# A fused attention and expert kernel, closed by a block without GpSimd's drain

## The chip, the cores and the metric

The kernel runs on one core of a Trainium2 chip. Times are device microseconds (us) of one execution. Three runs of the kernel before took 154.77, 157.05 and 154.83 us, median 154.83 us. A further execution was taken with the hardware profiler.

## What is computed

Tokens x (64 sequences of 64 tokens, 128 wide, f32) go through one gated cross-attention step and one gated mixture-of-experts step:

```python
x = x + tanh(g_xattn[0]) * xattn(layernorm(x), ctx, ctx, Wq, bq, Wk, bk, Wv, bv)
x = x + tanh(g_ffn[0]) * ffn(layernorm(x), Wr, br, W1, W2)
# ffn, for each token h: route = sigmoid(h @ Wr + br); e = argmax(route)
#                        out = max(route) * (gelu(h @ W1[e]) @ W2[e])
```

There are 8 experts with W1 of 128 x 512 and W2 of 512 x 128, and each token goes to one of them.

## The kernel before, in words

The program is written engine by engine, with explicit semaphores, inside one block (`block = stack.enter_context(nc.Block())`). Within the block each of the five engines has its own instruction list: SyncE (SP) issues loads, ScalarE (ACT) and VectorE (DVE) do activations, copies and normalisation, TensorE (PE) does the matmuls, and GpSimd (POOL) does small vector operations and all the indirect DMAs. The 4096 tokens are 32 tiles of 128 rows, in 8 groups of 4.

In the first part each group is normalised, attends, and is routed; GpSimd then writes each of its 4 tiles into a DRAM buffer `scratch`, sorted by expert, with an indirect DMA (`scatter_rows`, line 408, 32 of them). In the second part 39 expert tiles are loaded back from `scratch` by SP, pass through two matmul layers, and GpSimd writes each finished tile to its rows of the output with an indirect DMA (`scatter_tile`, line 433, 39 of them; each adds 16 to the semaphore `tok_out`). Between two of these indirect DMAs GpSimd executes `pause()`, a memset of an unused tile (line 427). Nothing follows the last `scatter_tile` in GpSimd's list.

The last instruction in SP's list is a wait for all 39 output DMAs:

```python
            sp.wait_ge(tok_out, 16 * FFN_TILES)
```

Behind the lists the block closes. In the kernel before, each engine there branches to a common end, executes a DRAIN, and passes a barrier of all engines made of semaphore events. The profile puts these instructions down to line 74, the `with ExitStack() as stack:` that closes the block. A similar barrier stands at the program's start (line 1276). No computation comes behind the block.

Of the kernel before, what the change touches and what calls it, by code (L numbers as in the profile page):

```python
# [31 lines left out]
def attention_moe(nc, x, ctx_in, g_xattn, g_ffn, Wq, bq, Wk, bk, Wv, bv, Wr, br, W1, W2, out):  # L32
# [41 lines left out]
    with ExitStack() as stack:  # L74
# [206 lines left out]
        def lead(j):  # L281
            return 3 if j < 7 else 2

        block = stack.enter_context(nc.Block())

        @block.sync
        def _(sp):
# [999 lines left out]
```

## Time and profile before

| | |
|---|---|
| median of 3 runs | 154.83 us |
| lowest and highest run | 154.77 and 157.05 us |
| the profiled execution's own time | 155.01 us |
| its span, first to last instruction | 153.1 us |
| time of that execution outside its span | 1.91 us |
| mean granted TensorE clock | 0.975 |

The profile is one execution. Busy times count the work of an engine's datapath; an instruction that only the engine's sequencer executes (branch, semaphore event, DRAIN) is not counted as busy, and is listed with a q behind the engine's name (POOLq, SPq, PEldq). Where one line is queried, each row gives the shortest, median and longest duration of an instruction in ns and the start of the first and the last in us from the start of the span. A row of the chain of waits gives start, duration and instruction.

### The profile page before, as it was taken

To read this page: it belongs to the slowest core of one execution; us is meant where nothing else is said; L and a number is where in the kernel's file an instruction comes from. 1 tells how busy PE (TensorE), PEld (TensorE's weight loads), DVE (VectorE), ACT (ScalarE), POOL (GpSimd) and SP (SyncE) were. 2 spreads that over 40 slices of the span, in tenths; PEclk is the share of its full clock that TensorE was granted. 3 is DMA by queue.
4 is the path that set the end of the run, shared out by engine and by line. 5 is a ranking of instruction groups with operands and counts; after the bars stand their busy time and mean duration, and the time that the engine had idled before them with its cause. 6 is when DMAs were issued, how large, how long until landed. Compare 5 with 4: busy or idle time off the path is not lost.

```text
span 153.1 us, 4237 instructions
## 1 busy us (share of the span) xinstructions
PE 128.3 (84%) x1225; PEld 114.4 (75%) x1225; DVE 96.4 (63%) x542; ACT 77.7 (51%) x174; POOL 126.0 (82%) x209
## 2 busy tenths in 40 slices
PE   5999989998987958697599999999999999996000
PEld 5877856875774938697589998999999999995000
DVE  0699999879999997897198454454554454542000
ACT  0657397668658472628225555456546555431000
POOL 6539996898987988798989989989899898998930
PEclk9999999999999999999999999999999999999955
DMA  4999999631111241411243144544110101111000
GB/s 111 251 279 275 333 330 295 188 103 42 35 35 40 61 101 39 107 35 57 72 106 94 35 125 124 122 125 111 51 39 22 50 17 55 35 36 35 0 0 0
DMA packets 20080, 15.20 MB, mean 99 GB/s; under 512 B 6606, under 2 KB 16978, under 8 KB 20058
## 3 DMA queue, kind: packets, MB, share of 16 engines
q1 hardware_dynamic: 17328, 10.59, 26.5%
q0 software_dynamic: 2272, 4.27, 8.3%
q8 instruction: 11, 0.18, 0.5%
q10 hardware_dynamic: 458, 0.08, 0.3%
q14 instruction: 11, 0.09, 0.2%
HBM read 10.12 MB, written 5.26 MB: 100 GB/s over the span
## 4 chain that ended last, share of the span: by engine, by line
PE 43%; POOL 36%; issue 6%; DVE 5%; DMA 3%; ACT 1%; SPq 1%; POOLq 0%; DVEq 0%
PE banks_o L1172 20%; POOL scratch L408 15%; PE banks_v L1163 9%; POOL unused L427 6%; POOL rows L404 5%; PE bank_q L1163 5%; PE bank_p L1163 4%; POOL xn L369 3%; POOL out_dram L433 3%; POOL mv L362 3%; PE bank_x L1155 3%; PE bank_s L1039 2%; DMA scratch<-rows,row_at 1%; DMA tok<-scratch 1%; DVE stats L587 1%
## 5 line engine op out<-in xcount | busy, mean ns | idle before, releaser
L1172 PE MATMUL banks_o<-w_sb,hT 128*128 x312 | 41.8, 277 | 0.7 <-issue 0.5
L1172 PEld LDWEIGHTS banks_o<-w_sb,hT 128*128 128x128 f32 x312 | 37.9, 192 | 1.7 <-issue 1.6
L408 POOL DMA_INDIRECT scratch<-rows,row_at x32 | 31.8, 994 | 5.7 <-issue 5.0
L905 DVE SCALAR_TENSOR_TENSOR tok<-banks_o,tok 128x128 f32<-128x128 f32 x39 | 13.6, 348 | 29.6 <-PE banks_o L1172 29.2
L427 POOL MEMSET unused<- 128x400 f32 x64 | 29.4, 459 | 0.1
L480 ACT COPY w_now<-w_sb 128x512 f32 x39 | 23.7, 612 | 4.6 <-issue 4.6
L433 POOL DMA_INDIRECT out_dram<-tok,token_at x22 | 21.6, 982 | 3.7 <-issue 3.2
L1163 PE MATMUL banks_v<-toknT,w_now 128*128 128x128 f32 x160 | 21.1, 275 | 0.0
L894 DVE TENSOR_SCALAR tokn<-tok 128x128 f32<-128x128 f32 x39 | 18.4, 472 | 2.9 <-DMA tok<-scratch 2.9
L1163 PEld LDWEIGHTS banks_v<-toknT,w_now 128*128 128x128 f32 x160 | 19.4, 192 | 0.0
L433 POOL DMA_INDIRECT out_dram<-tok x17 | 16.7, 982 | 2.9 <-issue 2.4
L537 ACT ACTIVATE hT<-banks_v 128x512 f32<-128x512 f32 x20 | 12.0, 598 | 13.8 <-PE banks_v L1163 13.8
L1155 PE MATMUL bank_x<-ident,tokn 128*128 128x128 f32 x39 | 11.0, 283 | 4.9 <-DVE tokn L894 3.9
L901 DVE COPY toknT<-bank_x 128x128 f32<-128x128 f32 x39 | 11.2, 286 | 1.3 <-PE bank_x L1155 1.3
L362 POOL TENSOR_TENSOR mv<-mv,minus_half 128x4 f32<-128x4 f32 x8 | 8.2, 1020 | 4.6 <-DVE mv L595 4.6
L677 DVE SCALAR_TENSOR_TENSOR rows<-banks_o,inv_sum,x_all 128x136 f32<-128x136 f32 x32 | 10.9, 352 | 0.0
L404 POOL TENSOR_TENSOR rows<-rows,minus_half 128x4 f32<-128x4 f32 x8 | 8.3, 1040 | 2.9 <-DVE rows L742 2.7
L1163 PE MATMUL bank_q<-toknT,w_now 128*128 128x128 f32 x80 | 10.6, 276 | 0.0
L524 ACT ACTIVATE probs<-bank_s,minus_max 128x64 f32<-128x64 f32 x32 | 7.4, 315 | 5.9 <-DVE minus_max L641 5.9
L537 ACT ACTIVATE hT<-bank_q 128x512 f32<-128x512 f32 x10 | 5.9, 593 | 8.4 <-PE bank_q L1163 8.4
L1155 PEld LDWEIGHTS bank_x<-ident,tokn 128*128 128x128 f32 x39 | 5.6, 142 | 6.1 <-DVE tokn L894 6.0
L1163 PEld LDWEIGHTS bank_q<-toknT,w_now 128*128 128x128 f32 x80 | 9.7, 192 | 0.0
(162 smaller groups left out, 252.9 us busy)
## 6 DMA issues: line engine op xcount, KB each, us to landing
tok<-scratch SPq DMA_DIRECT2D x39, 66.0 KB, 2.1
x_all<-in_x_dram SPq DMA_DIRECT2D x8, 256.0 KB, 4.5
w_sb<-in_L_ffn_W_dram SPq DMA_DIRECT2D x1, 2048.0 KB
ctx<-in_ctx_dram SPq DMA_DIRECT2D x8, 128.0 KB, 4.5
scratch<-pad_rows SPq DMA_DIRECT2D x1, 528.0 KB, 19.5
scratch<-rows,row_at POOLq DMA_INDIRECT x32, 2.4
out_dram<-tok,token_at POOLq DMA_INDIRECT x22
out_dram<-tok POOLq DMA_INDIRECT x17
```

What stands on the lines that cost most here:

```text
L362: nc.gpsimd.tensor_tensor(rstd, var, minus_half[:].unsqueeze(2), ALU.pow).then_inc(rstd1_ready, 1)
L404: nc.gpsimd.tensor_tensor(column(g, RSTD), column(g, RSTD), minus_half[:].unsqueeze(2), ALU.pow).then_inc(rstd2_ready, 1)
L408: nc.gpsimd.indirect_dma_start(out=scratch, out_offset=bass.IndirectOffsetOnAxis(ap=row_at[:, g * GT + t:g * GT + t + 1], axis=0), in_=row ...
L427: nc.gpsimd.memset(unused[:], 0.0).then_inc(paused, 1)
L433: nc.gpsimd.indirect_dma_start(out=out_tok, out_offset=bass.IndirectOffsetOnAxis(ap=at, axis=0), in_=tok[j][:, 0:D], in_offset=None, bound ...
L480: nc.scalar.copy(w1_now[j % DEEP][:], w1_sb[:, bass.ds(w_at[j], F)]).then_inc(w1_copied, 1)
L537: nc.scalar.activation(hT[j % DEEP][:], h_ps[j % DEEP], ACT.Gelu).then_inc(gelu_done, 1)
L894: nc.vector.tensor_scalar(tokn[j % 2][:], tok[j][:, 0:D], tok[j][:, MEAN:RSTD], tok[j][:, RSTD:SCALE], ALU.subtract, ALU.mult).then_inc(to ...
L905: nc.vector.scalar_tensor_tensor(out=tok[j][:, 0:D], in0=y_ps[j % 2], scalar=tok[j][:, SCALE:TOKEN], in1=tok[j][:, 0:D], op0=ALU.mult, op1 ...
L1155: nc.tensor.transpose(tT_ps, tokn[j % 2][:], ident[:]).then_inc(toknT_done, 1)
L1163: last = nc.tensor.matmul(h_ps[j % DEEP][:, c * P:(c + 1) * P], w1_now[j % DEEP][:, c * P:(c + 1) * P], toknT[j % DEEP][:], start=True, st ...
L1172: last = nc.tensor.matmul(y_ps[j % 2], hT[j % DEEP][:, c * P:(c + 1) * P], w2_sb[:, bass.ds(w_at[j] + c * D, D)], start=(c == 0), stop=(c ...
```

## The change

The block is built with an option that leaves out GpSimd's DRAIN at its end. The other four engines still drain, and the engines still meet in a barrier of semaphore events. The lists of instructions inside the block stay as they are.

```diff
-        block = stack.enter_context(nc.Block())
+        block = stack.enter_context(nc.Block(no_gpsimd_drain=True))
```

## Rows read from the trace of the kernel before

**Rows 1.** The page: its head, and each engine's busy time, share and instructions.
```profile
span 153.1 us, 4237 instructions
...
PE 128.3 (84%) x1225; PEld 114.4 (75%) x1225; DVE 96.4 (63%) x542; ACT 77.7 (51%) x174; POOL 126.0 (82%) x209
```

**Rows 2.** Busy time of each engine in three stretches at the end.
```profile
core 0: us, PE busy (x) PEld busy (x) DVE busy (x) ACT busy (x) POOL busy (x), PEclk, DMA share, GB/s
136.00:139.20 3.20, 3.20 (x30) 3.14 (x29) 0.55 (x5) 1.19 (x2) 2.86 (x5) 1.00 0.15 46
139.20:147.00 7.80, 0.99 (x8) 0.80 (x8) 0.77 (x3) 0.00 (x0) 6.95 (x10) 0.89 0.03 7
147.00:153.10 6.10, 0.00 (x0) 0.00 (x0) 0.00 (x0) 0.00 (x0) 0.00 (x0) 0.50 0.00 0
```

**Rows 3.** The chain that ended last, from 139.2 us on.
```profile
139.20 0.36 DVE tok L905
...
139.63 0.98 POOL out_dram L433
...
145.40 0.45 POOLq L74
...
146.02 0.98 POOL out_dram L433
```

**Rows 4.** Line 74, the closing of the block: every instruction kind by engine.
```profile
L74 POOLq EVENT_SEMAPHORE  x2: 17/17/17, 152.9 to 153.0; - x2
L74 ACTq DRAIN  x1: 627/627/627, 138.3 to 138.3; - x1
L74 PEldq DRAIN  x1: 805/805/805, 139.4 to 139.4; - x1
L74 DVEq DRAIN  x1: 391/391/391, 140.2 to 140.2; - x1
L74 POOLq DRAIN  x1: 8050/8050/8050, 144.8 to 144.8; - x1
L74 SPq COMPARE_BRANCH  x1: 45/45/45, 148.2 to 148.2; - x1
L74 SPq DRAIN  x1: 13/13/13, 148.4 to 148.4; - x1
L74 SPq EVENT_SEMAPHORE  x1: 17/17/17, 153.0 to 153.0; - x1
...
L74 PEldq EVENT_SEMAPHORE  x1: 51/51/51, 153.1 to 153.1; - x1
```

**Rows 5.** DMA traffic from 147 to 149 us, in 40 slices of 0.05 us.
```profile
GB/s 0 0 0 0 0 0 0 0 0 0 0 0 5 2 4 1 0 0 0 0 0 0 0 0 0 0 0 0 0 0 0 0 0 0 0 0 0 0 0 0
DMA packets 32, 0.00 MB, mean 0 GB/s; under 512 B 32, under 2 KB 32, under 8 KB 32
```

**Rows 6.** What SP's queue waited for from 147 us on: total, times, longest.
```profile
SPq L74 <- DMA out_dram<-tok,token_at: 43.3, 1, 43.3
SPq L74 <- PEq L74: 4.7, 1, 4.7
```

**Rows 7.** GpSimd's indirect DMAs by line, and the time to landing of those to scratch.
```profile
L433 POOL DMA_INDIRECT out_dram<-tok,token_at x22: 980/980/1020, 112.4 to 146.0; - x22
L433 POOL DMA_INDIRECT out_dram<-tok x17: 980/980/997, 85.3 to 110.8; - x17
...
L408 POOL DMA_INDIRECT scratch<-rows,row_at x32: 967/967/1191, 28.3 to 83.5; - x32
...
DMA to landing us min/median/max: 2.3/2.4/3.7
```

**Rows 8.** Line 1276, the barrier at the start.
```profile
L1276 POOLq DRAIN  x1: 187/187/187, 0.3 to 0.3; - x1
...
L1276 SPq EVENT_SEMAPHORE  x1: 17/17/17, 0.7 to 0.7; - x1
```

**Rows 9.** GpSimd's waits before the output scatters: total, times, longest.
```profile
POOL out_dram L433 <- issue: 5.6, 33, 0.2
```

## The prediction

> **What bounds the kernel now.** I read the page's head first, then asked what stands between the last busy instruction and the end of the span, because the change touches only the closing of the block. GpSimd is busy for 126.0 of 153.1 us [rows 1], which alone says nothing about the end. The stretches say more. From 136.0 to 139.2 us TensorE is busy throughout; from 139.2 to 147.0 us GpSimd alone has much to do (6.95 of 7.80 us); from 147.0 to 153.1 us no engine's datapath does anything, for 6.10 us [rows 2]. The chain confirms the hand-over: the last tile's VectorE add ends at 139.56 us, and from there it is one GpSimd output scatter after another until the last one, which runs from 146.02 to 147.00 us [rows 3].
>
> The silent 6.1 us are read from line 74, and the reader should put its rows in order of time [rows 4]. ACT, PE and DVE drain at 138.3, 139.4 and 140.2 us and are done by 140.6 us. GpSimd's sequencer starts its DRAIN at 144.8 us, ahead of its own datapath, which still has two scatters to finish. The DRAIN lasts 8.05 us, so until 152.85 us. Meanwhile the last output packets move at 147.60 to 147.80 us (slices 13 to 16 of the view) [rows 5], SP's wait for all 39 output DMAs ends, and SP branches at 148.2 us and drains at 148.4 us in 13 ns [rows 4]. SP then waits 4.7 us at the barrier [rows 6]. The profile names PEq as what released it, but PE had drained by 140.2 us; the two semaphore events of GpSimd at 152.9 and 153.0 us, right behind its DRAIN, are what everybody waits for [rows 4]. So the end of the span is set by GpSimd's DRAIN, and the next to arrive behind it is SP.
>
> **The change part by part.** One thing is removed: a DRAIN of 8.05 us on GpSimd's sequencer. Its parts are 2.15 us from 144.85 to 147.00 us, beside the scatters; 1.42 us from 147.00 to 148.42 us, beside the landing of the last output DMA and SP's branch and DRAIN; and 152.85 - 148.42 = 4.43 us beside nothing [rows 3, 4]. The first two are hidden and stay: SP's wait covers them, since it needs every output DMA. Only the third leaves the path.
>
> What is late next is SP, at 148.42 us. Behind the last arrival the barrier took 153.10 - 152.85 = 0.25 us before [rows 1, 4]; the barrier at the start took about the same, from the end of GpSimd's DRAIN at 0.49 us to the semaphore event of SP at 0.7 us [rows 8]. The new span is 148.42 + 0.25 = 148.67 us, 4.43 us less.
>
> The order of the barrier may change, which the trace before doesn't show. Its nearest rows are the events of 17 to 51 ns and the steps of about 0.1 us between GpSimd's two events and the others' [rows 4]. From below I allow 0.2 us less, if GpSimd's events are ready sooner; from above five engines in series at 0.1 us, 0.5 us, which is 0.25 us more. I take no difference, because both barriers shown took about 0.25 us.
>
> GpSimd's list inside the block has the same instructions, so the 39 scatters of 0.98 us and what precedes them stay where they are [rows 7]. Moving nothing costs nothing; a gain inside the block is excluded too, since the DRAIN stands behind all of it.
>
> Outside the span the profiled execution has 155.01 - 153.1 = 1.91 us. What is in it isn't shown. From below it stays; from above the whole 4.43 us comes back in it. I take it as unchanged, because the row nearest to an operation at that place, SP's DRAIN at the end, takes 13 ns [rows 4], and the DRAIN of GpSimd at the start 187 ns with four memsets under it [rows 8].
>
> The sum is 155.01 - 4.43 = 150.58 us for an execution like the profiled one. That one lies 0.18 us above the median of 154.83 us, so on the median's scale it is **150.4 us**, 2.9% less. The error of the rounded starts is 0.1 us.
>
> **Why the DRAIN lasts past the landing** decides the rivals. With no indirect DMA before it, it took 187 ns [rows 8]; with 32 + 39 = 71 of them before it, it ended 5.85 us after the last scatter's end [rows 3, 4, 7] and over 5 us after the last packet [rows 5]. So it is not waiting for data. It does something for the DMAs behind it, 4.43 / 71 = 62 ns each if it goes by their number. Nobody in this program uses the result.
>
> **Rival 1: the cost comes back behind the block.** The work is owed, and whatever closes the execution must do it, or GpSimd's cores are really occupied until 152.85 us and the barrier's event waits for them, drain or none. Then the time stays at 154.8 us. For it: the DRAIN is long after all data has landed [rows 4, 5], so somebody found it worth doing. Against it: GpSimd's sequencer ran 1.2 us ahead of its last scatter (144.8 against 146.02 us) [rows 3, 4], so an instruction of the sequencer doesn't wait for the cores, and the 1.91 us outside have no room in which 4.43 us are already being paid. Half of it may return, at 152.6 us.
>
> The Trainium skill's page "VectorE: DVE Perf Modes", section "The DRAIN you can't avoid", speaks against this change: it says that the runtime's preamble and postamble contain DRAINs of their own on all five engines, of some 12 ns each. If GpSimd's inherits the debt, the time is 154.8 us; if it takes 12 ns, 150.4 us. No row here lies behind the block, so the trace can't tell. The skill's page "Runtime: NRT & Kernel Launch", section "The ~15µs preamble/postamble breakdown", puts 9 to 15 us around a kernel in all; only 1.91 us are outside the span here, so by that page most of the postamble would be outside this metric too, and a debt paid there would not be seen.
>
> **Rival 2: slower, because the next execution pays.** Its place is GpSimd's scatters. Without the DRAIN the bookkeeping of 71 DMAs is left for the next execution, whose scatters must then clear it, one by one, on the engine that ends the kernel [rows 2, 3]. The waits named issue before the output scatters are 0.17 us each (5.6 us over 33) [rows 9]. If each of 71 scatters paid as much again, that is 12.1 us on the path: 150.4 + 12.1 = 162.5 us. It ends more than 2% slower than before from (4.43 + 3.1) / 71 = 0.106 us each. Against it: the scatters are steady at 980 ns, the highest 1020 [rows 7], although the number outstanding since the last DRAIN grows from 1 to 71 within the run; a cost that grows with the debt would show already.
>
> **Rival 3: the drain is put in anyway** by a later step of the build, and nothing changes: 154.8 us. Nothing in the profile speaks for or against it.
>
> **How the numbers follow.** My forecast, 150.4 us, has 0.76, with a range of its own from 149.8 to 151.1 us: the barrier's bounds of -0.2 and +0.25 us, 0.1 us of rounding, and some 0.3 us by which two sets of runs may differ. Rival 1 in full has 0.13, with a part of the cost returned (up to 152.6 us) 0.05. Rival 3 has 0.02 and rival 2 0.04. The range of 8 in 10 takes in the forecast and the partial return, from 149.7 to 152.6 us, and leaves out 0.19. About 2%, 3.1 us, is what a measurement tells from no change here; faster by over 2% means below 151.7 us. The forecast lies there almost whole, and of the partial return a fifth: 0.77. Within 2% are rival 1 in full, most of its part and rival 3: 0.19. Slower 0.04.
>
> **What would show it.** In the changed kernel's trace line 74 has no DRAIN of POOLq; GpSimd's first semaphore event may stand before 148.4 us; SP's wait for another engine at the barrier falls from 4.7 us to under 0.3 us; the stretch without work behind the last scatter shrinks from 6.1 to about 1.7 us; the span is 148.7 us and what lies outside it still 1.9 us. If the span falls and the outside grows, rival 1 is right in its form outside; if GpSimd's semaphore event starts near 152.9 us, in its form on the cores. If scatters or the waits before them lengthen, rival 2. What would make the prediction wrong without any of these is a last output DMA that lands later than 2.4 us after its start, the median of the scatters shown [rows 7].

## The result, and the profile after

The changed kernel took 0.971 of the time of the kernel before, with a 95% interval of 0.966 to 0.976: 2.9% faster, where 2.9% was forecast. Its median over 7 runs is 151.22 us against 157.05 us for the kernel before in its 7. Both sets contain executions in which the whole program ran longer, the changed kernel's profiled one among them; the ratio compares the others of each, 149.85 to 151.44 us for the changed kernel. The spans of these are 148.1 to 149.6 us, where 148.7 us was forecast.

In the profiled execution of the changed kernel (156.78 us, span 155.0 us, mean granted clock 0.952) everything up to the last scatter lies later than in [rows 3]. So absolute times are not compared; the tail is read from the end of GpSimd's last scatter. The last lines of the chain, and the two stretches on either side of that end:

```profile
151.75 0.45 POOL unused L427
152.20 0.17 issue
152.37 0.98 POOL out_dram L433
```

```profile
core 0: us, PE busy (x) PEld busy (x) DVE busy (x) ACT busy (x) POOL busy (x), PEclk, DMA share, GB/s
145.56:153.35 7.79, 0.82 (x8) 0.63 (x6) 0.60 (x3) 0.00 (x0) 6.94 (x10) 0.82 0.03 7
153.35:155.01 1.66, 0.00 (x0) 0.00 (x0) 0.00 (x0) 0.00 (x0) 0.00 (x0) 0.50 0.01 0
```

The scatter ends at 153.35 us and the span 1.66 us later, where it was 6.10 us in [rows 2]: 4.44 us have gone. The closing of the block answers to [rows 4]:

```profile
L74 ACTq EVENT_SEMAPHORE  x2: 17/17/17, 145.2 to 154.9; - x2
L74 PEldq EVENT_SEMAPHORE  x2: 51/51/51, 146.5 to 154.9; - x2
L74 DVEq EVENT_SEMAPHORE  x2: 21/21/21, 146.9 to 154.9; - x2
L74 SPq EVENT_SEMAPHORE  x2: 17/17/17, 154.8 to 154.9; - x2
L74 POOLq EVENT_SEMAPHORE  x2: 17/17/17, 154.8 to 154.9; - x2
L74 ACTq DRAIN  x1: 627/627/627, 144.5 to 144.5; - x1
L74 PEldq DRAIN  x1: 720/720/720, 145.7 to 145.7; - x1
L74 DVEq DRAIN  x1: 389/389/389, 146.4 to 146.4; - x1
L74 SPq COMPARE_BRANCH  x1: 45/45/45, 154.5 to 154.5; - x1
L74 SPq DRAIN  x1: 13/13/13, 154.7 to 154.7; - x1
```

No DRAIN of POOLq is left. The others each execute two semaphore events instead of one: an arrival right behind their DRAIN (ACT at 145.2 us) and a release at 154.9 us. SP is last to arrive, at 154.8 us, 0.1 us behind its DRAIN. GpSimd's own first event comes right behind SP's and not earlier, although its last scatter had ended at 153.35 us, and the release follows at once. By this order GpSimd now waits for SP, where SP waited for GpSimd before. The waits of SP's queue answer to [rows 6], 4.7 us there:

```profile
SPq L74 <- DMA out_dram<-tok,token_at: 45.7, 1, 45.7
SPq L74 <- PEq L74: 0.2, 1, 0.2
```

Outside the span lie 156.78 - 155.0 = 1.78 us, and between 1.75 and 1.88 us in all seven runs, against 1.91 us before. The scatters keep their length, 980 ns in the median as in [rows 7]:

```profile
L433 POOL DMA_INDIRECT out_dram<-tok,token_at x22: 980/980/1000, 118.8 to 152.4; - x22
L433 POOL DMA_INDIRECT out_dram<-tok x17: 980/980/997, 91.6 to 117.2; - x17
```

The DRAIN that GpSimd executes at the program's start takes what it took in [rows 8], 187 ns there:

```profile
L1276 POOLq DRAIN  x1: 188/188/188, 0.3 to 0.3; - x1
```

### The profile page after: what moved, and what is told of

It reads as the page before. It is cut to its first block, busy times and chain, and to the rows that moved or that the text cites. A ratio compares the mean times of both kernels' runs of the same rounds, so it can differ in the third digit from the quotient of the medians.

```text
span 155.0 us, 4240 instructions
## 1 busy us (share of the span) xinstructions
PE 135.8 (88%) x1225; PEld 122.3 (79%) x1225; DVE 97.0 (63%) x542; ACT 78.1 (50%) x174; POOL 126.3 (82%) x209
## 3 DMA queue, kind: packets, MB, share of 16 engines
q0 software_dynamic: 2272, 4.27, 8.2%
## 4 chain that ended last, share of the span: by engine, by line
PE 39%; POOL 35%; DVE 13%; issue 8%; DMA 3%; SPq 1%; POOLq 0%; DVEq 0%
POOL scratch L408 15%; PE banks_o L1172 14%; POOL unused L427 8%; POOL out_dram L433 7%; PE banks_v L1163 7%; POOL rows L404 5%; PE bank_q L1163 3%; PE bank_p L1163 3%; PE bank_s L1039 3%; DVE stats L587 3%; PE bank_x L1155 2%; DMA scratch<-rows,row_at 2%; DVE rows L677 1%; DVE mv L591 1%; PE bank_x L1062 1%
## 5 line engine op out<-in xcount | busy, mean ns | idle before, releaser
L905 DVE SCALAR_TENSOR_TENSOR tok<-banks_o,tok 128x128 f32<-128x128 f32 x39 | 13.6, 348 | 30.0 <-PE banks_o L1172 29.2
L1163 PE MATMUL banks_v<-toknT,w_now 128*128 128x128 f32 x160 | 22.4, 286 | 0.0
L1163 PEld LDWEIGHTS banks_v<-toknT,w_now 128*128 128x128 f32 x160 | 20.8, 203 | 0.0
L894 DVE TENSOR_SCALAR tokn<-tok 128x128 f32<-128x128 f32 x39 | 17.6, 456 | 2.8 <-DMA tok<-scratch 2.8
L537 ACT ACTIVATE hT<-banks_v 128x512 f32<-128x512 f32 x20 | 11.9, 597 | 13.6 <-PE banks_v L1163 13.6
L1092 PE MATMUL banks_v<-wvg_sb,ctxT 65*128 65x137 f32 x64 | 9.9, 302 | 0.0
```

What stands on the lines that cost most here:

```text
L537: nc.scalar.activation(hT[j % DEEP][:], h_ps[j % DEEP], ACT.Gelu).then_inc(gelu_done, 1)
L894: nc.vector.tensor_scalar(tokn[j % 2][:], tok[j][:, 0:D], tok[j][:, MEAN:RSTD], tok[j][:, RSTD:SCALE], ALU.subtract, ALU.mult).then_inc(to ...
L905: nc.vector.scalar_tensor_tensor(out=tok[j][:, 0:D], in0=y_ps[j % 2], scalar=tok[j][:, SCALE:TOKEN], in1=tok[j][:, 0:D], op0=ALU.mult, op1 ...
L1163: last = nc.tensor.matmul(h_ps[j % DEEP][:, c * P:(c + 1) * P], w1_now[j % DEEP][:, c * P:(c + 1) * P], toknT[j % DEEP][:], start=True, st ...
```

## The experiments

All ratios are to the kernel before, on the same chip, with 95% intervals in brackets. Most of these intervals are too wide to tell a difference of 2% from none, so the argument rests on the traces beside them. Where a time is given more finely than a row of line 74 shows it, it is the trace's own time, which that view rounds to 0.1 us.

### The changed kernel again

No edit. 

> The changed kernel once more, for a trace to set beside the one before. My theory (GpSimd's DRAIN alone stood on the path, for 4.4 us behind SP's arrival, and nothing is owed for it later): about 150.4 us, a ratio of 0.971 to the kernel before; span about 148.7 us, outside it 1.9 us; SP's last wait under 0.3 us; scatters at 967 and 980 ns as before. Rival 1 (the cost returns behind the block): outside the span over 2.5 us. Rival 2 (the next execution pays): scatters longer than 980 ns or more than 0.17 us of wait before each.

 Measured: ratio 0.9735 (0.9589 to 0.9882); SP's last wait 0.2 us; outside the span 155.73 - 153.9 = 1.83 us.

> The changed kernel again, beside the two below on one chip. Ratio to the kernel before 0.970 to 0.973; in its trace SP's last wait is 0.2 us and the span ends 0.3 us behind SP's DRAIN.

 Measured on another chip: ratio 0.9671 (0.9598 to 0.9745). Its scatters and the idle time before the output scatters:

```profile
L433 POOL DMA_INDIRECT out_dram<-tok,token_at x22: 977/977/982, 116.4 to 149.8; - x22
...
  issue: 5.4, 32
```

The last scatter ends at 150.80 us and the span at 152.4 us, 1.6 us later. 5.4 / 32 = 0.17 us of wait before each scatter, as in [rows 9], and a DRAIN of 188 ns at the start again. None of the 17 executions in the three sets of the changed kernel is near the 162.5 us of rival 2, the longest being 157.54 us. So no sign of a later execution that pays was found, which speaks against rival 2; the record doesn't say which kernel ran on the core just before each execution. With 1.83 us outside the span rival 1 has nothing for it either. A cost paid outside the device time altogether would not be seen in any run here.

### The drain put back by hand

```diff
+            nc.gpsimd.drain()
```

The line is the last in GpSimd's list; the block stays without a drain of its own. 

> The block without GpSimd's drain, but GpSimd's own list ends with an explicit drain: the same DRAIN back, with the barrier of the changed kernel. If the DRAIN is the whole cause: it lasts about 8.05 us from 144.8 us and the time returns to about 154.8 us, ratio 1.00 to the kernel before (within 0.003). If the form of the barrier, or the place of the code behind the block, brought the gain: the time stays at about 150.4 us, ratio 0.97.

 Measured: ratio 0.9999 (0.9891 to 1.0107). The changed barrier is still there, with two events on each engine, the gain is not. The DRAIN, and SP's waits beside it:

```profile
L453 POOLq DRAIN  x1: 8043/8043/8043, 148.7 to 148.7; - x1
```

```profile
SPq L74 <- DMA out_dram<-tok,token_at: 43.8, 1, 43.8
SPq L74 <- PEq L74: 4.6, 1, 4.6
```

It lasts 8.04 us and SP waits 4.6 us again. So the DRAIN is the cause: SP's wait comes back to within 0.1 us of the 4.7 us before, and the time to within the 1.1% of its interval.

### Two drains in a row

```diff
+            nc.gpsimd.drain()
```

This is added to the kernel before, whose block has its own drain. 

> The kernel before with an explicit drain at the end of GpSimd's list, so two DRAINs stand behind one another. If the DRAIN does work for DMAs issued since the last one: the first lasts about 8.05 us, the second under 0.2 us, and the time is 155 us, ratio 1.00. If a DRAIN has a fixed cost once GpSimd has issued indirect DMAs: the second costs another 4.4 to 5.9 us, and the time is 159 to 161 us, ratio 1.03 to 1.04.

 The first DRAIN (line 453) and the block's own (line 74):

```profile
L453 POOLq DRAIN  x1: 8043/8043/8043, 149.6 to 149.6; - x1
```

```profile
L74 POOLq DRAIN  x1: 41/41/41, 157.6 to 157.6; - x1
```

The second takes 41 ns. So the price is not a fixed one that every DRAIN pays once GpSimd has issued indirect DMAs; it works off what came since the last one. No ratio came out; two of its runs, 158.33 and 159.83 us, lie within or just above the 156.75 to 158.98 us of the kernel before, not 3 to 4% above as with a second full DRAIN.

### The drain only after everything has landed

```diff
+            pool.wait_ge(tok_out, 16 * FFN_TILES)
+            nc.gpsimd.drain()
```

> As own_drain, but GpSimd waits for all 39 output DMAs on their semaphore before its drain, so the DRAIN starts only when everything has landed, at about 148.2 us. If its work begins at the landing of the last DMA: it lasts about 4.5 us and ends near 152.8 us, time 154.8 us, ratio 1.00. If its work begins when GpSimd's cores are free (147.0 us): it lasts about 5.9 us and ends near 154.1 us, time 156.1 us, ratio 1.008. If it can run beside the scatters from 144.8 us on: it lasts about 8 us, time 158.3 us, ratio 1.02.

 Measured: ratio 1.006 (1.0001 to 1.012), which leaves out the 1.02 of work beside the scatters and hardly tells the other two apart. The trace does:

```profile
L454 POOLq DRAIN  x1: 5872/5872/5872, 152.0 to 152.0; - x1
```

This DRAIN has nothing to wait for: no scatter is in GpSimd's cores, every DMA has signalled. It still takes 5.87 us. In the kernel before the same 5.88 us (5.85 by the rounded rows) ran from the last scatter's end at 147.00 us, the first 1.4 of them beside the landing and SP's branch and DRAIN. That is the price of the DRAIN's own work here, and it doesn't wait for data.

### How it grows: drains in the middle

```diff
                 scatter_rows(g, t)
+                if at in (7, 31):
+                    nc.gpsimd.drain()
```

This is added to the kernel before, in the loop over its 32 scatters to scratch. 

> The kernel before with two more drains in GpSimd's list, behind the 8th and the 32nd scatter to scratch, so that 8, 24 and 39 indirect DMAs stand before the three DRAINs. Read from the end of the last scatter to the end of the DRAIN, which was 5.85 us with 71 before it. If its work goes by the number of DMAs since the last DRAIN (62 ns each behind a landing 1.4 us after the scatter): about 1.9, 2.9 and 3.8 us. If it is fixed: 5.9 us all three times. If it goes by all DMAs since the program's start: 1.9, 3.4 and 5.9 us.

 

> The kernel before with one more drain behind the 29th output scatter, so that 61 indirect DMAs stand before it and 10 before the DRAIN at the end. Work by the number since the last DRAIN: 5.2 us and 2.0 us from the end of the scatter to the end of the DRAIN. Fixed: 5.9 us twice. By all DMAs since the start: 5.2 and 5.9 us.

 The second kernel drains behind output scatter 29 (`if j == 28`). Their DRAINs, first of drains behind 8 and 32, then of the drain behind 29:

```profile
L446 POOLq DRAIN  x2: 5226/5414/5601, 38.1 to 87.7; - x2
...
L74 POOLq DRAIN  x1: 5396/5396/5396, 153.3 to 153.3; - x1
```

```profile
L452 POOLq DRAIN  x1: 7225/7225/7225, 132.6 to 132.6; - x1
...
L74 POOLq DRAIN  x1: 3760/3760/3760, 153.9 to 153.9; - x1
```

Each DRAIN starts early, so its scatters must be taken off. For the one at 132.6 us, for instance, the timeline shows GpSimd's last scatter before it and the pause behind it (start, duration, idle time before):

```profile
133.83 0.98 POOL L433 DMA_INDIRECT out_dram<-tok,token_at  x1 [0.17 <-issue]
139.94 0.43 POOL L427 MEMSET unused<- 128x400 f32 x1 [5.13 <-issue]
```

The scatter ends at 134.81 us and the DRAIN at 139.87 us (132.6 + 7.225 with its start rounded): 5.06 us, and the pause starts 0.07 us later. The two drains in the first part, in the same view:

```profile
41.02 0.96 POOL L408 DMA_INDIRECT scratch<-rows,row_at  x1 [0.17 <-issue]
43.75 0.43 POOL L427 MEMSET unused<- 128x400 f32 x1 [1.77 <-issue]
```

```profile
89.39 1.17 POOL L408 DMA_INDIRECT scratch<-rows,row_at  x1 [0.17 <-issue]
92.98 0.43 POOL L427 MEMSET unused<- 128x400 f32 x1 [2.42 <-issue]
```

At the block's end the last scatters are these, first with 39 and then with 10 DMAs since the last DRAIN:

```profile
154.44 0.98 POOL out_dram L433
```

```profile
155.05 0.98 POOL out_dram L433
```

| DMAs since the last DRAIN | us from last scatter's end to DRAIN's end | ns per DMA |
|---|---|---|
| 8 | 1.70 | 212 |
| 10 | 1.60 | 160 |
| 24 | 2.35 | 98 |
| 39 | 3.24 | 83 |
| 61 | 5.06 | 83 |
| 71 (before; own_drain; two_drains) | 5.88; 5.88; 5.88 | 83 |

From 39 DMAs on the work is in proportion to their number: 83 ns each, with nothing fixed beside it. Neither a fixed price nor the count since the start (71 at the end in both kernels) fits 3.24 and 1.60 us. Below that the DRAIN takes longer than 83 ns each, by 0.4 us at 24 and by 0.8 to 1.0 us at 10 and 8. With 8 and 10 it ends 0.8 us behind the last packet of the last scatter (42.91 and 156.83 us; the DRAINs end at 43.68 and 157.63 us), so it probably waits for landing when its own work is shorter. With 24 it ends 1.4 us behind it (91.48 and 92.91 us), and the extra 0.4 us has no explanation here. Each of these five counts was seen in one trace.

### DMAs or rows

```diff
-                    ... IndirectOffsetOnAxis(ap=at, axis=0), in_=tok[j][:, 0:D] ...
+                    ... IndirectOffsetOnAxis(ap=at[0:64], axis=0), in_=tok[j][0:64, 0:D] ...
```

This kernel leaves half of the output unwritten, and ran once. 

> As landed_first (GpSimd waits for its output DMAs, then drains), but every output scatter moves only the first 64 of its 128 rows, so half of the output is left unwritten. The number of DMAs before the DRAIN stays 71, their rows fall from 71 x 128 to 51.5 x 128. From the five DRAINs so far the work is about 0.45 us and 0.075 us per DMA of 128 rows. If it goes by DMAs: the DRAIN lasts 5.9 us again. If it goes by rows (descriptors): 0.45 + 51.5 x 0.075 = 4.3 us.

 Measured:

```profile
L454 POOLq DRAIN  x1: 5872/5872/5872, 145.5 to 145.5; - x1
```

5.872 us to the nanosecond, though GpSimd's queue moved 3.18 instead of 4.27 MB. It goes by the number of DMAs, not by their rows. Both kernels show 2272 packets on that queue, 32 per DMA, so it may as well be the packets; DMAs with another number of packets weren't tried.

### What bounds the end now: the pauses

```diff
-                if j < FFN_TILES - 1:
+                if j < 30:
                     pause()
```

> The changed kernel without GpSimd's pauses behind output scatters 30 to 37 (8 memsets of 0.47 us of an unused tile, with about 0.14 us of semaphore work each). With the DRAIN gone GpSimd's scatters are the last work, at 1.60 us each, 5 of them behind the last tile's add at 139.56 us. If they are the bound: the last scatter can start at 139.7 us plus at most one or two of 1.0 us, so the end comes 4 to 5 us earlier, time 145.5 to 146.5 us, ratio 0.94 to 0.95. If scatters without a pause between them become longer (their descriptors or the queue limit them at 1.6 us): time unchanged at 150.4 us, ratio 0.97.

 Measured: ratio 0.9624 (0.9512 to 0.9735), a smaller gain than I expected, and its interval overlaps that of the changed kernel, 0.966 to 0.976. The chain shows why. These are its four last scatters; the second number is the part of a scatter that the chain counts, not its length.

```profile
144.52 0.20 POOL out_dram L433
...
145.80 0.71 POOL out_dram L433
...
147.23 0.30 POOL out_dram L433
...
148.52 0.98 POOL out_dram L433
```

They start 1.28 to 1.43 us apart, not the 1.0 us of a scatter's own length. Dropping a pause saves about 0.3 us of the 1.60 us step, not 0.6 us, so eight save some 2.5 us at most.

With all 38 gone between the output scatters: 

> The changed kernel without any of the 38 pauses between output scatters. The last tile's add at 139.56 us then sets the end: last scatter at 139.7 us, landing 2.4 us later at 142.1 us, span 142.6 us, time about 144.5 us, ratio 0.93. If the pauses shelter VectorE or the DMA rings from GpSimd's scatters, the adds come later and the time lies between 145 and 151 us.

 Measured: ratio 0.9416 (0.9286 to 0.9546). For the second set: 

> The kernel without the 38 pauses between output scatters once more, to narrow its interval, 0.929 to 0.955 in the first set. If GpSimd's backlog at the end is the bound behind the DRAIN, the ratio is about 0.945, that is 2.5 to 3% below the changed kernel's on the same chip. If the first set was chance, the two are alike at 0.97.

 It gave no ratio of its own, so the interval was not narrowed. Its lowest run was 145.46 us, the changed kernel's lowest on that chip 149.93 us. GpSimd's groups from 80 us on, with their idle time, in the first set, and the end of its chain:

```profile
L433 POOL DMA_INDIRECT out_dram<-tok,token_at x22 | 21.5, 978 | 15.4 <-DVE tok L903 13.6 <-issue 1.8
L433 POOL DMA_INDIRECT out_dram<-tok x17 | 16.7, 982 | 5.1 <-issue 4.6 <-DVE tok L903 0.5
```

```profile
140.06 0.36 DVE tok L903
...
141.21 0.30 POOL out_dram L433
141.51 0.98 issue
142.49 0.98 POOL out_dram L433
```

GpSimd now waits 13.6 us for VectorE's adds in the last 22 scatters, so it has caught up; the last add ends at 140.42 us and only one scatter, at 141.21 us, still stands between it and the last. The backlog of [rows 3], 6.5 us between the last add and the last scatter's start, has become 2.1 us.

```diff
                 if at in RSTD2_AT:
                     rstd2(RSTD2_AT[at])
-                else:
-                    pause()
```

With the first part's pauses gone too: 

> The changed kernel without any pause, also those between the 32 scatters to scratch (26 more memsets of 0.47 us). If GpSimd bounds the first part as well, these 26 at about 0.3 us each come off partly: ratio 0.92 to 0.94. If the groups' arrival (VectorE's routing work) sets the times of the scatters to scratch, or VectorE is hindered by denser scatters: no better than without the output pauses, ratio 0.94 to 0.96.

 Measured: ratio 0.9439 (0.9345 to 0.9534), no better than without the output pauses alone. In the first part GpSimd waits for VectorE instead, 9.0 us before this group, against 2.7 us with the first part's pauses in place (first set above):

```profile
L404 POOL TENSOR_TENSOR rows<-rows,minus_half 128x4 f32<-128x4 f32 x8 | 8.3, 1037 | 9.1 <-DVE rows L738 9.0
```

Both versions beat the changed kernel by about 3% in the ratios (0.942 and 0.944 against 0.967 to 0.974). The intervals are wide and no direct ratio was formed, but that of the version without any pause, 0.935 to 0.953, lies clear of the changed kernel's on the same chip, 0.960 to 0.975.

## Why the prediction was right

**What bounds.** Right: GpSimd's DRAIN set the end. Put back by hand it brings the time back (0.9999, 0.989 to 1.011) and SP's wait of 4.6 us, and the barrier's new form brings nothing that this could show.

**The saving of 4.43 us.** Right: the tail behind the last scatter went from 6.10 to 1.66 us, 4.44 us less. The two parts of the DRAIN taken as hidden, 2.15 us beside scatters and 1.42 us beside the last landing, stayed in the tail or before it. The working has a slip that doesn't touch the sum: the row of the DRAIN starts at 144.8 us, so the first part is 2.2 us, and only then do the three parts make 8.05 us. That forecast and measurement agree to the digit in 2.9% is luck; the interval of the measurement is 2.4 to 3.4%.

**The barrier.** Taken as 0.25 us, it is 155.0 - 154.71 = 0.3 us, with one event more on each engine but GpSimd. The bounds held. The sign that GpSimd's first event might stand before 148.4 us didn't show: in every trace of the changed kernel it comes right behind SP's, as the last.

**Nothing inside the block moves.** Right for the lists and the length of the scatters.

**Outside the span nothing comes back.** Right, as far as the device time reaches: 1.75 to 1.88 us. The rule in the Trainium skill's page "VectorE: DVE Perf Modes", section "The DRAIN you can't avoid", that the postamble's own DRAINs take some 12 ns, agrees with the time that was measured; whether GpSimd has one there no run here shows.

**What the DRAIN does.** The mis-sized part. I spread the 4.43 us that stuck out over 71 DMAs, 62 ns each, as if the work began after the landing. It begins when GpSimd's cores are free, 1.4 us earlier, and is 5.87 us in all: 83 ns each. That also corrects the reading that an instruction of the sequencer doesn't wait for the cores: the DRAIN starts beside the scatters, but its work doesn't. The sum didn't depend on it. What the work is for stays open; the runs show only by what it grows.

**The rivals.** Rival 1 fell in both forms: GpSimd's first event at the barrier comes about 1.5 us behind its last scatter's end and not 5.9, and the outside did not grow. Against rival 2 stand 0.17 us before each scatter and 188 ns for the DRAIN at the start, as before, and times that all stayed short of it. Rival 3 fell: line 74 has no DRAIN of POOLq.

## What to carry to other kernels

Look at what stands between the last busy instruction and the end of the span, and put the sequencers' rows there in order of time: here only the DRAIN of the engine that arrived last cost time, and the gain ended where the next one, SP, arrived. This kernel has a semaphore wait for all output DMAs in SP's list, and could close without GpSimd's DRAIN. An estimate for one like it, from the table: 83 ns for each indirect DMA since the last drain (seen with 39 to 71 of them), counted from the last scatter's end, less what lies before the next engine's arrival; here 71 x 83 ns = 5.9 us less 1.4 us. A kernel that leaves more than 71 DMAs without a drain wasn't tried. When the end is freed so, read the backlog in front of it next; here the pauses in it were worth about as much again.

## What the runs showed that was not expected

A DRAIN of GpSimd took 5.872 us for 71 indirect DMAs that had all landed, and 5.872 us again when 39 of them were half as large, 83 ns each; a second one right behind a full one took 41 ns. Indirect DMAs whose own rows in the profile last 0.98 us followed one another no closer than 1.28 us, and with a memset of 0.47 us between them 1.60 us, so the memset cost 0.32 us of its 0.47.
